# Attention heads in the two row halves of the array, one value bank, and a new split of the expert work over the engines

## The reference

```
q, k, v = x @ Wq.T + bq, x @ Wk.T + bk, x @ Wv.T + bv      # 16 heads of 8
scores = einsum("bqhd,bkhd->bhqk", q, k) * attn_scale      # masked by position,
attn = softmax(where(mask, -inf, scores))                  # in chunks of 64
x = layernorm(x + (attn @ v) @ Wo.T + bo)
scores = sigmoid(x @ gate_w.T)                             # 32 experts
combine = top 6 of the experts in the best 4 of 8 groups, weights normed to 2.5
routed = sum_e combine[:, e] * ((silu(x @ Wg_e.T) * (x @ Wu_e.T)) @ Wd_e.T)      # I = 64
x = layernorm(x + routed + shared expert(x))                                     # I = 128
```

## Time and profile before

| | |
|---|---|
| time, median of 3 runs | 520.54 us (520.14 to 521.09) |
| span of the profiled execution | 514.3 us |
| time outside the span (the difference) | 6.2 us |
| PE, DVE, ACT, POOL busy | 468.9, 402.1, 263.1, 216.8 us |
| TensorE's clock, mean over the span | 0.936 of 2.4 GHz |

### The profile page before, as it was taken

How to read it: one execution, slowest core, us unless ns; L and a number is a source line. 1 busy time by engine, 2 the same in 40 slices (tenths; PEclk the granted TensorE clock), 3 DMA queues, 4 the chain that set the end, 5 groups by cost and what they waited for, 6 DMA issues and landing times.

```text
span 514.3 us, 8899 instructions
## 1 busy us (share of the span) xinstructions
PE 468.9 (91%) x3212; PEld 259.2 (50%) x3212; DVE 402.1 (78%) x780; ACT 263.1 (51%) x375; POOL 216.8 (42%) x260
## 2 busy tenths in 40 slices
PE   5899799999999999999999997898988898899872
PEld 1474233444434444443434553686765576667651
DVE  7809977788887878788786457699889889968963
ACT  4510035666656676665576766444564464545440
POOL 9100033625345362544413323455644556655561
PEclk9955559999999999999999999899999999999996
DMA  4444110020211203020000000633222253452320
GB/s 138 154 145 134 59 34 15 7 88 20 73 39 31 66 19 83 26 65 32 3 2 3 1 1 2 138 109 92 83 82 82 83 112 96 120 135 83 102 82 20
DMA packets 23340, 34.22 MB, mean 67 GB/s; under 512 B 5121, under 2 KB 13186, under 8 KB 22530
## 3 DMA queue, kind: packets, MB, share of 16 engines
q1 hardware_dynamic: 23106, 33.41, 22.7%
q10 hardware_dynamic: 192, 0.26, 0.2%
HBM read 29.00 MB, written 4.46 MB: 65 GB/s over the span
## 4 chain that ended last, share of the span: by engine, by line
PE 59%; DVE 16%; issue 10%; POOL 10%; ACT 3%; DMA 2%; SPq 1%; DVEq 0%; POOLq 0%; ACTq 0%
PE ps L1082 15%; PE ps L1039 13%; PE ps L1064 12%; POOL hlo L615 8%; DVE mx L758 6%; DVE hh L983 3%; PE ps L1042 3%; DVE au L978 2%; PE ps L1013 2%; PE ps L1010 2%; PE ps L1149 2%; PE ps L1151 2%; PE ps L1150 2%; POOL rstd L588 1%; PE ps L1176 1%
## 5 line engine op out<-in xcount | busy, mean ns | idle before, releaser
L758 DVE TENSOR_REDUCE mx<-ps 128x1 f32<-128x512 f32 (+3 forms) x304 | 189.7, 660 | 45.4 <-PE ps L1042 37.6
L660 ACT ACTIVATE probs<-ps 128x1024 f32<-128x1024 f32 (+4 forms) x176 | 147.8, 869 | 110.8 <-PE ps L1064 110.4
L615 POOL TENSOR_TENSOR hlo<-hh,hhi 128x512 fp32r<-128x512 f32 x68 | 91.4, 1351 | 90.6 <-ACT hhi L715 85.3
L1039 PE MATMUL ps<-rows_k,rows_q 72*128 72x512 bf16 (+3 forms) x384 | 123.8, 365 | 2.1 <-DVE mx L758 0.9
L570 POOL TENSOR_SCALAR_AFFINE_SELECT probs<-probs 64x512 f32<-64x512 f32 x64 | 42.4, 662 | 127.1 <-ACT probs L660 126.1
L1082 PE MATMUL ps<-probs,Vg 128*32 128x256 f32 (+1 forms) x1280 | 92.9, 370 | 0.0
L1064 PE MATMUL ps<-rows_q,rows_k 99*128 99x512 bf16 (+3 forms) x384 | 92.3, 334 | 0.0
L1039 PEld LDWEIGHTS ps<-rows_k,rows_q 72*128 72x128 bf16 x384 | 37.5, 103 | 81.7 <-DVE mx L758 53.5
L983 DVE TENSOR_TENSOR hh<-rows_k,au 128x512 f32<-128x512 f32 x64 | 71.4, 1115 | 5.8 <-DMA rows_k<-weights 3.6
L726 ACT ACTIVATE sg<-ps 128x512 f32<-128x512 f32 x68 | 40.7, 598 | 55.7 <-PE ps L1151 54.1
L978 DVE TENSOR_TENSOR au<-ps,sg 128x512 f32<-128x512 f32 x64 | 43.7, 683 | 19.2 <-POOL hlo L615 10.5
(11 more groups left out here) (115 smaller groups left out, 479.5 us busy)
## 6 DMA issues: line engine op xcount, KB each, us to landing
rows_k<-weights SPq DMA_DIRECT2D x128, 128.0 KB, 3.0
w_raw<-in_unitT SPq DMA_DIRECT2D x17, 192.0 KB, 12.4
scratch<-oT SPq DMA_DIRECT2D x8, 384.0 KB, 2.9
rows_q<-scratch SPq DMA_DIRECT2D x8, 192.0 KB
rows_k<-scratch SPq DMA_DIRECT2D x8, 192.0 KB
xT<-in_xT SPq DMA_DIRECT2D x4, 256.0 KB, 4.4
rows_q<-scratch SPq DMA_DIRECT2D x8, 128.0 KB
rows_k<-scratch SPq DMA_DIRECT2D x8, 128.0 KB
```

Source lines behind the costliest of these rows:

```text
L615: pool.tensor_tensor(hlo[:, i % 2, :], hh[:, i % 2, :], hhi[:, i % 2, :], ALU.subtract).then_inc(hidden_low, 1)
L660: act.activation(dst, src, ACT.Exp).then_inc(exps_ready, 1)
L758: dve.tensor_reduce(mx[:, part, j:j + per, qt], src, AX.X, ALU.max).then_inc(max_read, 1)
L1039: mm = pe.matmul(bank(max_bank(g, n), m, at), q, rows_k[0:K_MAX, s, j * T + k0:j * T + k0 + m], start=True, stop=part == 1)
```

## The change

**Row halves.** `rows_q` and `rows_k` hold two heads on partitions 0 to 63 and two on 64 to 127, 48 rows each and 3 for the maxima behind them (`ROWS`, `K_EXP` = 51, `ROW_HALF` = 64). An exponential unit issues two products, one in each half, into neighbouring banks. Maxima units take the halves in turn, in a ring of three banks. The mask of a diagonal square is two products of 64 columns through a 64-row matrix `pick`. `load_rows` issues 12 transfers of half the size in place of 6, and the store of the maxima 6 in place of 3.

**Blocks and one value bank.** Exponentials and values go through 12 blocks of a group (`BLOCKS`), each one key tile against one half (512) of the queries, in four slots of `probs`; all value products go to bank 4, which ACT copies out twice a group. The transposed maxima are copied by ACT (`copy_tops`) and split by GpSimd in 5 steps; the transpose is placed behind the fourth maxima unit of the next group. `attention_order()` now writes out an order for GpSimd too (masks, splits, weights), which SP follows with its transfers.

**Start.** The bias of v is added by GpSimd in `values`, not by a one-row product; half of the v products move into the sequence of the maxima (`V_AT`). Projections use four banks. The clearing of the row buffers shrinks to one fill of `rows_k` a slot, on GpSimd. ACT issues 8 small transfers for `pick` and the mask first.

**Experts.** Three steps in flight (`FLIGHT`). GpSimd multiplies silu by the router's weights; DVE makes one product with up and, one step later, the low part.

```diff
-ROWS_QK = 48
-MROW = 96
-K_MAX = 72
-K_EXP = MROW + 3
+ROWS = 48
+K_EXP = ROWS + 3
+ROW_HALF = P // 2
...
+BLOCKS = [(0, 7), (0, 3), (0, 6), (0, 2), (0, 5), (0, 1), (0, 4), (0, 0), (1, 7), (1, 6), (1, 5), (1, 4)]
...
+        units += [(b, (0, 1), n)] if 2 * n <= BANK else [(b, (0,), n), (b, (1,), n)]
...
-    hop, rows_latency, load = 240, 5500, 6000
-    LEAD = 1.5
+    hop, rows_latency, load = 240, 3500, 6000
+    LEAD = 1.6
...
-            t += per * P * (kt + 2) / 2.4
+            t += len(pairs) * (m / 2.4 + 60)
...
+                    part = scr[which, b, :, r, :].rearrange("h (d f p) t -> f h d (p t)", d=D, f=2)
+                    for f in range(2):
+                        if reps is None:
+                            spans = ((0, 24, part[f]), (24, 16, part[f, 0:2]), (40, 8, part[f, 0]))
+                        else:
+                            spans = ((0, 24, part[f, 0:1].to_broadcast([3, D, PAIRS * T])),
+                                     (24, 16, part[f, 1:2].to_broadcast([2, D, PAIRS * T])), (40, 8, part[f, 2]))
+                        for at, n, src in spans:
+                            sp.dma_start(dst[ROW_HALF * f + at:ROW_HALF * f + at + n, s, :],
+                                         src).then_inc(rows_loaded[s], 16)
...
+            def split_top(g):
+
+
+                pool.wait_ge(tops_copied, g + 1)
+                if g >= 1:
+                    pool.wait_ge(max_rows_loaded[(g - 1) % NS], 96 * ((g - 1) // NS + 1))
+                pool.tensor_scalar(mh[:, 0, :], tops[:, :], -1.0, None, ALU.mult).then_inc(max_split_steps, 1)
+                pool.wait_ge(max_split_steps, 3 * g + 1)
+                pool.tensor_tensor(mr[:, :], tops[:, :], mh[:, 0, :], ALU.add).then_inc(max_split_steps, 1)
+                pool.wait_ge(max_split_steps, 3 * g + 2)
+                pool.tensor_scalar(mh[:, 1, :], mr[:, :], -1.0, None, ALU.mult).then_inc(max_split_steps, 1)
+                pool.wait_ge(max_split_steps, 3 * g + 3)
+                pool.tensor_tensor(mr[:, :], mr[:, :], mh[:, 1, :], ALU.add).then_inc(max_rest, 1)
+                pool.wait_ge(max_rest, g + 1)
+                pool.tensor_scalar(mh[:, 2, :], mr[:, :], -1.0, None, ALU.mult).then_inc(max_split, 1)
 
             def split_unit(u):
...
-                low_part(i)
+                if i % NU:
+                    p = pairs(i)
+                    pool.wait_ge(silu_ready, i + 1)
+                    pool.wait_ge(comb_rows_loaded[p % CB], 32 * (p // CB + 1))
+                    if i >= FLIGHT:
+                        pool.wait_ge(hidden_ready, i - FLIGHT + 1)
+                    pool.tensor_tensor(sgc[:, i % FLIGHT, :], sg[:, i % FLIGHT, :], comb_rows[:, p % CB, :],
+                                       ALU.mult).then_inc(weighted_ready, 1)
             root(*ROOT_AT[NC * NU], QUAD)
 
...
-                dve.wait_ge(silu_ready, i + 1)
+                if i:
+                    low_part(i - 1)
                 dve.wait_ge(ups_ready, i + 1)
-                if i >= 2:
-                    dve.wait_ge(hidden_low, i - 1)
+                if i >= FLIGHT:
+                    dve.wait_ge(hidden_low, i - FLIGHT + 1)
                 if u:
-                    dve.tensor_tensor(au[:, i % 2, :], bank(2 + i % 2), sg[:, i % 2, :],
-                                      ALU.mult).then_inc(gated_ready, 1)
-                    dve.wait_ge(gated_ready, pairs(i + 1))
-                    p = NPAIR * n + u - 1
-                    dve.wait_ge(comb_rows_loaded[p % CB], 32 * (p // CB + 1))
-                    dve.tensor_tensor(hh[:, i % 2, :], comb_rows[:, p % CB, :], au[:, i % 2, :],
-                                      ALU.mult).then_inc(hidden_ready, 1)
+                    dve.wait_ge(weighted_ready, pairs(i + 1))
                 else:
-                    dve.tensor_tensor(hh[:, i % 2, :], bank(2 + i % 2), sg[:, i % 2, :],
-                                      ALU.mult).then_inc(hidden_ready, 1)
+                    dve.wait_ge(silu_ready, i + 1)
+                dve.tensor_tensor(hh[:, i % FLIGHT, :], up_bank(i), (sgc if u else sg)[:, i % FLIGHT, :],
+                                  ALU.mult).then_inc(hidden_ready, 1)
+            low_part(NC * NU - 1)
             for step in (0, 1, 2, 4):
                 second_norm(NC - 1, step)
 
...
-                    q = rows_q[0:K_MAX, s, j * T + qt * P:j * T + (qt + 1) * P]
-                    mm = pe.matmul(bank(max_bank(g, n), m, at), q, rows_k[0:K_MAX, s, j * T + k0:j * T + k0 + m],
-                                   start=True, stop=part == 1)
+                    f, p = ROW_HALF * (j // PAIRS), j % PAIRS * T
+                    mm = pe.matmul(bank(b, m, at), rows_q[f:f + ROWS, s, p + qt * P:p + (qt + 1) * P],
+                                   rows_k[f:f + ROWS, s, p + k0:p + k0 + m], start=True, stop=part == 1)
                     if part == 0:
-                        mm = pe.matmul(bank(max_bank(g, n), P, at), identb[:, :], mask_qk[:, :], start=False,
-                                       stop=True)
+                        for c in range(2):
+                            mm = pe.matmul(bank(b, CHUNK, at + c * CHUNK), pick[f:f + CHUNK, c, :],
+                                           mask_k[f:f + CHUNK, :], start=False, stop=c == 1)
                 mm.then_inc(max_scores, 1)
...
+                for a_, p in enumerate(pairs):
+                    for f in range(2):
+                        r = slice(ROW_HALF * f, ROW_HALF * f + K_EXP)
+                        mm = pe.matmul(bank((NE * g + n) % 2 * 2 + f, m, a_ * m),
+                                       rows_k[r, s, p * T + kt * P:p * T + (kt + 1) * P],
+                                       rows_q[r, s, p * T + qh * BANK:p * T + qh * BANK + m], start=True, stop=True)
...
-            for h in range(2):
-                pe.wait_ge(output_copied[h], NG)
-            for i in range(NC * NU + 2):
+            pe.wait_ge(output_copied, QH * NG)
+            for i in range(NC * NU + FLIGHT):
                 if 2 <= i < NC * NU:
                     up(i)
                 if i in BACK_AT:
                     back(BACK_AT[i])
-                if i >= 2:
-                    down(i - 2)
+                if i >= FLIGHT:
+                    down(i - FLIGHT)
                 if i in TAIL_AT:
```

More of the change, by code:

```diff
@@ L53, in max_units @@
                 continue
-            per = BANK // m if BANK % m == 0 else 1
-            for j in range(0, HG, per):
-                units.append(([(j + a, qt, k0, m, a * m) for a in range(per)], m, part))
-    return units
+            heads = [(0, 1), (2, 3)] if 2 * m <= BANK else [(0,), (2,), (1,), (3,)]
+            units += [([(j, qt, k0, m, a * m) for a, j in enumerate(js)], m, part) for js in heads]
+    return units
+BLOCKS = [(0, 7), (0, 3), (0, 6), (0, 2), (0, 5), (0, 1), (0, 4), (0, 0), (1, 7), (1, 6), (1, 5), (1, 4)]
@@ L60, in exp_units, with width, masked @@
+QH = T // BANK
+HALF = KT // QH
+SLOTS = 4
+def width(b):
+    qh, kt = BLOCKS[b]
+    return min(BANK, P * (kt + 1) - BANK * qh)
+def masked(b):
+    qh, kt = BLOCKS[b]
+    return kt // HALF == qh
 def exp_units():
     units = []
[L64 to L72, removed]
+    for b in range(len(BLOCKS)):
+        n = width(b)
+        units += [(b, (0, 1), n)] if 2 * n <= BANK else [(b, (0,), n), (b, (1,), n)]
@@ L73, in exp_units @@
     return units
 MAXU, EXPU = max_units(), exp_units()
-NM = len(MAXU) + 1
+NM = len(MAXU)
 NE = len(EXPU)
[L79 to L92, removed]
@@ L93 @@
-PLACE_FROM = {kt: (0, kt + 2) if kt >= HALF else (0, HALF + 1 - PLACE[kt][0]) for kt in range(KT - 2)}
-PLACE_FROM.update({KT - 1: (-1, HALF - 2), KT - 2: (-1, 0)})
+NB = len(BLOCKS)
+EXPS_UP_TO = [sum(u[0] <= b for u in EXPU) for b in range(NB)]
+MASKS_UP_TO = [sum(masked(c) for c in range(b + 1)) for b in range(NB)]
+NMASK = MASKS_UP_TO[-1]
+HALF_END = {0: 7, 1: NB - 1}
+TOP_AFTER = 3
+MSEQ = []
+for g_ in range(NG):
+    for n_ in range(NM):
+        MSEQ.append(("unit", g_, n_))
+        if g_ and n_ == TOP_AFTER:
+            MSEQ.append(("top", g_ - 1, 0))
@@ L99 @@
+MSEQ.append(("top", NG - 1, 0))
+MAX_AT = {step: r for r, step in enumerate(MSEQ)}
+RING, RING0 = 3, 5
 QUAD = 4
+FLIGHT = 3
 TAIL = ([("out", 0, t) for t in range(QUAD)] + [("turn", 0, 0), ("proj", 0, 0)]
@@ L1014, in _, with max_step @@
                 mm.then_inc(v_projected, 1)
-            def max_unit(g, n):
+            for n in range(V_FIRST):
+                project_values(n)
+            def max_step(r):
+                kind, g, n = MSEQ[r]
                 s = g % NS
-                if n == 0:
-                    pe.wait_ge(rows_loaded[s], 96 * (g // NS + 1))
-                if g == 0 and n == 2:
+                if kind == "unit" and n == 0:
+                    pe.wait_ge(rows_loaded[s], 192 * (g // NS + 1))
+                if r == 0:
```

554 lines of the change are left out of this document (290 added, 264 removed).

## The result

The changed kernel took **503.82 us** (503.81 to 512.06, 5 runs) where the kernel before, on the same chip, took 521.09: 0.9682 of its time, 95% interval 0.9665 to 0.9700. The forecast was 475. The time is inside the range and the direction is right, but of 46 us forecast 17 came. The slowest of the five, 512.06, was a disturbed execution and is not in the ratio, and as it was the profiled one, the rows of after are from another execution of the same kernel, 501.45 us, from the runs of `after_again`. Every execution of these kernels took about 2.0 us more than its span, so the profiled execution of before, with a span of 514.3, stood for about 516.3.

A forecast was written before the change was run, and what follows sets the result against it. TensorE's order was taken to bound steady attention (30.35 us a group), a circle of TensorE and DVE the experts. 520.5 - 39 (attention) - 10 (experts) = 471.5, with 3 us for misplaced waits 475; range 456 to 508.

The forecast's parts named there:

- The mechanism of the halves: Attention on TensorE: exponential products paired in two row halves overlap, 4.6 us a group in place of 7.9.
- Rival 1: Attention: the row halves don't overlap, TensorE needs 28.9 us a group, result 501 (488 to 510); chance 0.20.
- TensorE's 24.5 us a group: Steady attention: TensorE's products sum to 24.5 us a group (21.5 to 28.5), 5.85 less than before.
- The start: Attention's start: maxima begin at 30 us, group 0 done at 52, first exponentials at 75, group 1 at 90.
- SP's queue: Attention's start: 12 us more transfer issue, added to a 21.09 us issue, delays first exponentials to 75 (68 to 79).
- six groups at 24.5: Attention after group 1: six periods, 147 us, end the last maxima at 237, 39 us earlier.
- 3 us for waits that the static order will misplace (split on GpSimd, weights queued behind 12-transfer loads): Allowance added to the sum for misplaced waits: 3 us, from 471.5 to 475.
- Rival 4, the clock: Steady attention: TensorE's clock falls with 48 or 51 row products; 538 at half the time, 598 wholly; chance 0.10.
- The tail: Batch 0's tail, from the end of the maxima to the experts' first silu: keeps its 43.4 us.
- the 12 us of cover: Batch 0's tail: a late E stream costs nothing until a cover of 12 us is gone.
- The experts: Experts: 68 steps of 2.3 us plus 20, 176 us against 186, so -10 (-20 to +8).
- The base: Starting time of the kernel before: 514.3 + 6.2 = 520.5 us, the median.

The follow-up runs named there:

- after_again: The changed kernel run again with no edit, for another profile: 505.23 us, ratio 0.962 to the kernel before.
- slot4_ahead: The changed kernel with a fourth slot for row copies and raw expert weights asked for two units ahead: 477.90 us, ratio 0.918 to before.
- raw4_v: The changed kernel with four raw weight buffers, loads three units ahead, and all v products before the maxima: 498.36 us, ratio 0.959 to before.
- raw4: The changed kernel with four raw weight buffers instead of two, loads three units ahead: 501.73 us, ratio 0.965 to before.
- raw4_fill: The kernel of raw4 with 22 unused full-height products put into each of TensorE's four waits for rows: 496.53 us, ratio 0.948 to before.
- plan13: The changed kernel with the planner's time for a row load at 13.6 us instead of 6.0: 506.78 us, ratio 0.971 to before.
- slot4_ahead_v: The kernel of slot4_ahead with all v products before the maxima: 475.77 us, ratio 0.912 to before.
- ahead_onehalf: The changed kernel with raw weights asked for two units ahead and every score product reading row half 0: 659.56 us, ratio 1.254 to before.
- bk48: The kernel before with maxima products over 48 of their 72 rows: 632.35 us, ratio 1.205 to before.

## Why the prediction was wrong, step by step

- **The mechanism of the halves: right.** Products of two halves run together: a pair in 0.23 us, 97.82 to 98.05, and a maxima product 0.01 us from an exponential one (timeline of PE, after).

```profile
97.82 0.39 PE L1142 MATMUL ps<-rows_q,rows_k 51*128 51x512 bf16 x2
98.05 0.38 PE L1119 MATMUL ps<-rows_k,rows_q 48*128 48x512 bf16 x1
98.27 0.22 PE L1123 MATMUL ps<-mask_k,pick 64*128 64x64 bf16 x2
...
101.58 0.39 PE L1119 MATMUL ps<-rows_k,rows_q 48*128 48x512 bf16 x1
101.59 0.39 PE L1142 MATMUL ps<-rows_q,rows_k 51*128 51x512 bf16 x1
```

  Rival 1 is out, although its sign came true: the joins of the changed kernel are 29.7 apart at the mean. TensorE's 24.5 us a group was a good size. In `slot4_ahead` the period is 24.05 in groups 2 and 3 and 25.65 in groups 4 to 7, 25.1 over the six, and TensorE is busy 24.3 of the 25.65 (its stretch of group 5):

```profile
161.04:186.70 25.66, 24.30 (x259) 9.60 (x257) 22.95 (x41) 18.80 (x24) 19.23 (x33) 1.00 0.24 73
```

  Of the 1.36 us that it idles there, 1.2 are waits for DVE's maxima, which are busy 22.95 and so nearly a bound too.
- **The start: too good by 7 us at group 0, made up at group 1.** The maxima began at 33.2 (I had 30), with two v products standing among them; group 0 ended at 59.2 (52), and at 55.6 with all v products ahead of the maxima (`raw4_v`). The first exponentials came at 69.2 (75), so group 1 ended at 86.8 (90). SP's queue cost less than I feared: wo's issue took 11.9 us, not 21.09.
- **The step that failed: "six groups at 24.5", with "3 us for waits that the static order will misplace (split on GpSimd, weights queued behind 12-transfer loads)".** The six took 178.1 us in place of 147, that is 31 more; the 3 was that term. I had named the mechanism and given it no working. The row load had doubled to 12 transfers, its rows usable 13.7 us behind the first request, and the period it had to hide in had shrunk by 6; I had TensorE's need and DVE's as the only bounds of a period, and never closed the circle of a slot (load, maxima, split, exponentials, load) or that of a raw weight buffer. An estimate from `slot4_ahead` shows how short the first is: group 4's rows are in use from 134.3 us, its first maxima, to 201.3, its last exponential product, 67 us; with 13.7 for the load that is 81, which three slots can turn round once in 27 us at best, four once in 20. `slot4_ahead`, which opens both circles and changes no product, has its join of group 7 at 238.0 (forecast 237) and 477.9 us. Over the six groups it takes 150.7: so of the 31 us, 27.4 were late transfers with what follows them, the fallen clock included, and 3.7 are left, which is less a need of TensorE's (busy 24.3 of 25.65) than its short waits for DVE.
- **Rival 4, the clock: half right, and misread.** I looked for it in the rows of the products at steady work; with both halves at work and no wait above 1.1 us the clock stayed at 1.00 (`slot4_ahead`). In `raw4` it fell in each of the four waits of 3.4 to 5.7 us, and with those filled it stayed up (`raw4_fill`), so these falls were a consequence of the late transfers, at 1.6 us a group. In the changed kernel each of its six falls from 98 to 255 us lies at a wait of 1.7 to 4.6 us. Some falls have less before them: in the changed kernel TensorE was idle for 1.9 us of 108 to 112, and the clock was 0.57 in the next 4 us; in `raw4` for 0.8 us of 96 to 100, and then 0.52. In `plan13` it was 0.43 us of 92 to 96, in waits of 0.28 at most, and then 0.58. In `slot4_ahead` 1.0 us of 236 to 240 changed nothing. What decides between them stays open, and with it whether every fall in the changed kernel was the late transfers' doing. The Trainium skill (TensorE: Matmul & The Clock Gate, A second HAM failure mode: psum-queue depth-cycling) has the clock swing where small gaps stand between groups of products. The traces agree in part: gaps of 0.15 to 0.28 us are all that stands ahead of the fall in `plan13`, while `slot4_ahead`, with 5.6 us of such gaps ahead of maxima units from 98 to 255 us, stayed at 1.00. Such gaps alone don't decide it.
- **The tail: too good by 6.** From the join of group 7 to the first silu it took 43.4 before, 49.6 after (264.8 to 314.4) and 49.5 in `slot4_ahead`. Batch 0's router kept its length: it ended at 308.8, 44.0 behind the join (before 42.5). What came later is the last output of the value stream, which ACT copies out just before it turns to the experts (timeline of ACT, first before, then after):

```profile
317.70 0.59 ACT L664 COPY oT<-ps 128x512 f32<-128x512 f32 x1 [4.59 <-PE ps L1082]
```
```profile
312.47 0.59 ACT L738 COPY oT<-ps 128x512 f32<-128x512 f32 x1 [5.30 <-PE ps L1159]
313.07 1.28 ACT L808 ACT_TABLE_LOAD   x1
314.37 0.60 ACT L808 ACTIVATE sg<-ps 128x512 f32<-128x512 f32 x1
```

  It starts 41.5 us behind the join before and 47.7 after, and that is the whole 6.1. So the 12 us of cover that I counted are not in the trace: before, too, this copy and not the router stood directly ahead of the first silu. That the value stream is longer because its exponentials lie further behind the maxima is not shown; no run separates it.
- **The experts: right.** First silu to last sum 176.6 us (314.4 to 491.0), forecast 176, before 185.7. DVE's low part behind ACT's cast is 846 ns at the mean, the product 683 (groups, 322 to 498 us):

```profile
L691 POOL TENSOR_TENSOR sgc<-sg,comb_rows 128x512 f32<-128x512 f32 x64 | 86.4, 1353 | 76.1 <-ACT sg L808 53.3 <-DMA comb_rows<-weights 19.8 <-DVE hh L1061 2.5
L1042 DVE TENSOR_TENSOR hlo<-hh,hhi 128x512 fp32r<-128x512 f32 x67 | 56.7, 846 | 28.2 <-ACT hhi L797 27.6
...
L1061 DVE TENSOR_TENSOR hh<-ps,sgc 128x512 f32<-128x512 f32 x64 | 43.7, 683 | 12.9 <-POOL sgc L691 12.9
...
L1253 PE MATMUL ps<-hhi,w_hi 128*128 128x512 f32 x68 | 28.3, 416 | 8.6 <-DVE hlo L1042 7.4 <-ACT moT L791 1.1
```

  The down products wait 7.4 us for the low part, where they waited 19.3 for GpSimd's.
- **The base.** I took 520.5 for an execution whose span was 514.3; by what all runs show outside the span it was 516.3.

The two profiled executions then add up: 514.3, less 11.4 at the join of group 7, plus 6.1 in the tail, less 9.1 in the experts, less 0.5 behind them, is 499.4, the span after.

`slot4_ahead_v`, with 475.77 us at 0.912 of before, beats both kernels. That it meets the forecast of 475 is partly luck. Its last maxima (236.0, forecast 237) and so its attention are as forecast, but its tail (50.2 us) and its experts (179.2) take 10 us more; a base taken 4.2 too high, the 3 for waits that it doesn't have, and the 1 at the last maxima nearly make that up.

## What to carry to other kernels

A stage that gets faster shortens the time in which its transfers can hide: for each buffer in a ring, add up load, use and release once with the new period, as for an engine. Two late transfers on one queue hide each other, and mending one alone may gain nothing (ratio 0.961) or lose (0.978) where both together bring 0.918. If a long wait on TensorE can't be removed, the clock behind it is a loss of its own, and filling the wait with products that nobody uses gave back 6.4 us in four groups here.

## What the runs showed of the hardware

- Products of 48 and 51 rows in one row half: busy 302 of 302 us at a granted clock of 0.50 (`ahead_onehalf`); in both halves, busy 191 of 204 us at 1.00 (`slot4_ahead`, 76 to 280). 48-row products between 99 and 128-row ones: busy 100 of 100 us at 0.50, and busy 90 of 90 at 1.00 later in the same execution (`bk48`).
- Two products of 51 rows and 512 columns, one in each row half, take 0.23 us together, as long as one. From a 48-row product to a 128-row one 0.10 us passes that 72 rows don't cost.
- SP issues a row transfer in 0.63 to 0.65 us in most loads; a load of 12 is usable 13.7 to 14.0 us after its first issue (`raw4`, four loads). The load of wo held SP for 11.9 us with 12 transfers to a group ahead of it and for 21.09 with 6.
- TensorE idle for 5.00 us, to 143.24: granted clock 0.51 in 144 to 148 and 1.00 in 148 to 152 (`raw4`). Idle for no more than 0.43 us of 92 to 96: 0.58 in 96 to 100 (`plan13`).
